# Rows and weights of a feed-forward stage brought in by the stage ahead of it, and its first layer put ahead of its global net

## What is computed

```python
x = x + attn_a(layernorm(x))     # phase A: holographic memory, prefix sums
x = x + ffn(layernorm(x))        # phase F, first time  ("f1")
x = x + attn_b(layernorm(x))     # phase B: hyperbolic Q and K, softmax attention
x = x + ffn(layernorm(x))        # phase F, second time ("f2"), same weights

def ffn(x):
    gf = global_net(x.mean(over rows))        # three small layers, per image
    out = x
    for _ in range(3):
        tf = coupling_net(out)                # 256 -> 256 -> 128 -> 64 -> 1, gelu between
        coupling = 0.1 + adaptive_range * (0.7 * gf + 0.3 * tf - 0.5) * 2
        out = out + coupling * twist(out)
    return out
```

## Time and profile before

| | us |
|---|---|
| three runs | 3031.08, 3026.36, 3031.05 (median 3031.05) |
| the profiled execution | 3026.34 |
| its span in the trace | 3024.6 |
| phase A | 0 to 934.8 |
| phase F, f1 | 934.8 to 1320.9 |
| phase B | 1320.9 to 2636.5 |
| phase F, f2 | 2636.5 to 3024.6 |
| busy: PE / ACT / DVE / POOL | 2724.5 / 2051.4 / 1865.1 / 1231.5 |

### The profile page before, as it was taken

How to read it: one execution, slowest core, us unless ns; L and a number is a source line. 1 busy time by engine, 2 the same in 40 slices (tenths; PEclk the granted TensorE clock), 3 DMA queues, 4 the chain that set the end, 5 groups by cost and what they waited for, 6 DMA issues and landing times. The chain is left out here.

```text
span 3024.6 us, 53754 instructions
## 1 busy us (share of the span) xinstructions
PE 2724.5 (90%) x20801; PEld 1241.0 (41%) x20801; DVE 1865.1 (62%) x2418; ACT 2051.4 (68%) x2696; POOL 1231.5 (41%) x755
## 2 busy tenths in 40 slices
PE   2799999999997999965999999999999999789997
PEld 1455555555554444322333333333333333244443
DVE  8899999999994445456455555555555441144444
ACT  6454454555433555546989898989999999755554
POOL 3788998888893122011414232323232220022100
PEclk7899999999998999977999999999999999999999
DMA  2000010101003021125445455455554546222112
GB/s 84 0 32 25 28 42 24 31 28 32 9 28 106 28 84 55 56 82 112 53 97 90 101 93 105 85 101 97 91 107 78 106 78 123 61 84 70 45 39 70
DMA packets 164051, 201.19 MB, mean 67 GB/s; under 512 B 16505, under 2 KB 118273, under 8 KB 163841
## 3 DMA queue, kind: packets, MB, share of 16 engines
q1 hardware_dynamic: 163840, 198.25, 29.3%
HBM read 139.49 MB, written 58.72 MB: 66 GB/s over the span
## 5 line engine op out<-in xcount | busy, mean ns | idle before, releaser
L1944 ACT ACTIVATE b_pr<-b_ps 128x1024 f32<-128x1024 f32 x1024 | 1000.2, 1035 | 99.2 <-PE b_ps L2012 93.3
L2012 PE MATMUL b_ps<-b_st 128*32 128x512 bf16 x8192 | 627.6, 381 | 43.3 <-ACT b_pr L1944 26.4
L2078 PE MATMUL b_acc<-b_pr,b_vaug 128*32 128x512 f32 x4096 | 542.0, 592 | 3.5 <-DVE b_osb L1773 3.2
L2012 PEld LDWEIGHTS b_ps<-b_st 128*32 128x32 bf16 x8192 | 186.9, 95 | 589.2 <-ACT b_pr L1944 355.0
L1257 PE MATMUL f_po<-f_s,f_w 128*128 128x512 f32 x768 | 353.5, 603 | 9.8 <-DVE f_xr L1042 6.0
L1030 DVE TENSOR_TENSOR f_turned<-f_cs,f_s 128x1024 f32<-128x1024 f32 x96 | 119.1, 1241 | 364.8 <-ACT f_cs L1159 359.3
L635 PE MATMUL a_pv<-a_xnT,a_wv 128*128 128x512 f32 x512 | 251.2, 614 | 52.9 <-DVE a_mem L403 38.7
L1123 ACT ACTIVATE f_h<-f_po,f_b 128x512 f32<-128x512 f32 x192 | 131.9, 687 | 217.0 <-PE f_po L1257 217.0
L627 PE MATMUL a_pu<-a_xnT,a_wk 128*128 128x512 f32 x512 | 238.5, 610 | 29.1 <-DVE a_frac L355 23.2
L1587 POOL TENSOR_TENSOR b_SQ<-b_A 128x1024 f32<-128x1024 f32 x28 | 58.3, 2082 | 438.3 <-DVE b_A L1698 438.3
L674 PE MATMUL a_py<-a_wo,a_out 128*128 128x256 f32 x960 | 229.1, 382 | 0.0
(11 more groups left out here) (283 smaller groups left out, 4545.1 us busy)
## 6 DMA issues: line engine op xcount, KB each, us to landing
b_st<-b_scratch SPq DMA_DIRECT2D x512, 128.0 KB, 7.2
b_scratch<-b_parts SPq DMA_DIRECT2D x32, 768.0 KB, 5.4
f_xl<-x SPq DMA_DIRECT2D x16, 1024.0 KB, 5.5
f_xr<-x SPq DMA_DIRECT2D x16, 1024.0 KB, 6.9
a_xl<-in_L_attn_a_x_dram SPq DMA_DIRECT2D x16, 512.0 KB, 4.3
x<-a_xr SPq DMA_DIRECT2D x32, 256.0 KB, 2.2
x<-f_xr SPq DMA_DIRECT2D x8, 1024.0 KB, 4.5
b_xl<-x SPq DMA_DIRECT2D x8, 1024.0 KB, 8.8
```

The source lines that it names most:

```text
L1944: nc.scalar.activation(pr[:, 4 * (blk % 2) + j, :], ps[:, j % 2, :], ACT.Exp, scale=SC).then_inc(S["probs_done"], 1)
L2012: x = nc.tensor.matmul(o[r:r + 32], w[:, r:r + 32], v, start=start, stop=stop, skip_group_check=True)
L2078: x = nc.tensor.matmul(acc[32 * j:32 * j + 32, h * 512:(h + 1) * 512], vaug[:, kt, c:c + 32], pr[:, 4 * (kt % 2) + j, h * 512:(h + 1) * 51 ...
```

## The change

One class (Front) with shared tiles stands for what a feed-forward stage needs at its start. Seven tiles are allocated once and used by all four phases: big (128 x 4 x 1024; wk_sb and wv_sb in phase A, A in phase B, xl in phase F), weights (128 x 2048; rnd and frac in phase A, EP in phase B, all the weights of phase F), ident, and stats, mv, sm and mhalf.

- **Phase A.** SP, once the last sine is done, issues the 18 loads of weights; once the last products of wk_sb and wv_sb are done, the two loads of rows (images 0 and 1 of x1, stored long before), and then waits for its last stores. DVE, behind L470, takes the statistics of both images and normalises them; POOL, behind its last sum, computes the scales.
- **Phase B.** In the program of the last image SP issues the two loads of rows and the 18 of weights, between the load of xr and the gather for g = 2. DVE takes the statistics in blocks 15 and 16, where the second lies between the two copies of take_acc, and normalises in blocks 21 and 22. POOL computes the scales.
- **Phase F.** Its loads, statistics, scales, normalisation and identity are gone. PE transposes, then does the first layer of image 0 (each tile waits only for the features that it reads and the bank that it writes), and then steps 0, 1 and 2 of the global net, ahead of the second layer. The barrier between the phases stays.
- ident is made once, in phase A; counts on setup_p are lowered for that.

```diff
@@ -51,6 +51,93 @@
...
+class Front:
...
+    def x(self, i):
+        v = self.big[:, 2 * i:2 * i + 2, :].rearrange("p a n -> p (a n)")
+        return v.rearrange("p (t d) -> p t d", t=8)
+
+    def load_rows(self, sp, rows):
+        for x in range(2):
+            sp.dma_start(self.x(x), rows[x]).then_inc(self.x_loaded[x], 16)
+
+    def load_weights(self, sp, loads):
+        for dst, src in loads:
+            sp.dma_start(dst, src).then_inc(self.w_loaded, 16)
+
+    def row_stats(self, nc, dve, x):
+        dve.wait_ge(self.x_loaded[x], 16)
+        for t in range(8):
+            nc.vector.bn_stats(self.stats[:, x, t, :], self.x(x)[:, t, :]).then_inc(self.stats_done, 1)
+        dve.wait_ge(self.stats_done, 8 * (x + 1))
+        for t in range(8):
+            nc.vector.bn_aggr(self.mv[:, x, t, :], self.stats[:, x, t, :]).then_inc(self.mv_done, 1)
+
+    def row_scales(self, nc, pool, x):
+        ve, rstd, nmean = (self.sm[:, i, x] for i in range(3))
+        pool.wait_ge(self.mv_done, 8 * (x + 1))
+        nc.gpsimd.tensor_scalar(ve, self.mv[:, x, :, 1], EPS, None, ALU.add).then_inc(self.rstd_done, 1)
+        nc.gpsimd.tensor_scalar(nmean, self.mv[:, x, :, 0], -1.0, None, ALU.mult).then_inc(self.rstd_done, 1)
+        pool.wait_ge(self.rstd_done, 3 * x + 1)
+        nc.gpsimd.tensor_tensor(rstd, ve, self.mhalf[:, 0:1].broadcast_to([P, 8]), ALU.pow).then_inc(self.rstd_done, 1)
+
+    def row_normalise(self, nc, dve, x):
+        dve.wait_ge(self.rstd_done, 3 * x + 3)
+        for t in range(8):
+            nc.vector.tensor_scalar(self.x(x)[:, t, :], self.x(x)[:, t, :], self.sm[:, 2, x, t:t + 1],
+                                    self.sm[:, 1, x, t:t + 1], ALU.add, ALU.mult).then_inc(self.xn_done, 1)
...
+def ffn_loads(w, cn, gc, arange):
...
+    return [(w["w1"], w1.rearrange("(k p) n -> p k n", p=P)), (w["b1"][:, 0:1], col(b1[0:P])), (w["b1"][:, 1:2], col(b1[P:2 * P])),
+            (w["w2"], w2.rearrange("(k p) n -> p k n", p=P)), (w["w3"], w3),
+            (w["gw1"], gw1.rearrange("(k p) n -> p k n", p=P)), (w["gw2"], gw2),
+            (w["w4c"][0:M3, :], w4), (w["w4c"][M3:P, :], w4), (w["gw3c"][0:M3, :], gw3), (w["b2"], col(b2)),
+            (w["b3"][0:M3, :], col(b3)), (w["b3"][M3:P, :], col(b3)), (w["gb1"], col(gb1)), (w["gb2"][0:M3, :], col(gb2)),
+            (w["sc"][:, 0:1], one(arange)), (w["sc"][:, 5:6], one(b4)), (w["sc"][:, 6:7], one(gb3))]
...
-def phase_a(nc, x_in, wk, wv, wo, gate, freqs, x_out):
+def phase_a(nc, x_in, wk, wv, wo, gate, freqs, x_out, nxt, nxt_loads):
...
-        wk_sb = s.sb("wk", [P, KD, HD])
-        wv_sb = s.sb("wv", [P, KD, HD])
+        wk_sb, wv_sb = nxt.big[:, 0:KD, :], nxt.big[:, KD:2 * KD, :]
...
-        ident = s.sb("ident", [P, P])
+        ident = nxt.ident
...
-        rnd = s.sb("rnd", [P, T])
-        frac = s.sb("frac", [P, T])
+        rnd, frac = nxt.weights[:, 0:T], nxt.weights[:, T:2 * T]
...
                 batch(B - 2)
+                sp.wait_ge(trig_done, NC * B)
+                nxt.load_weights(sp, nxt_loads)
+                sp.wait_ge(u_psum, NC * B)
+                sp.wait_ge(v_psum, 2 * NC * B)
+                nxt.load_rows(sp, [x_out[x].rearrange("(t p) d -> p t d", p=P) for x in range(2)])
...
                 batch(B - 1, last=True)
+                pool.wait_ge(half_done, 1)
+                for x in range(2):
+                    nxt.row_scales(nc, pool, x)
...
                 nc.vector.tensor_tensor(o, o, turn_v[:], ALU.add).then_inc(unit_done, 1)
+                for x in range(2):
+                    nxt.row_stats(nc, dve, x)
+                for x in range(2):
+                    nxt.row_normalise(nc, dve, x)
...
-def phase_f(nc, tag, x_in, x_out, cn, gc, arange):
-    w1, b1, w2, b2, w3, b3, w4, b4 = cn
-    gw1, gb1, gw2, gb2, gw3, gb3 = gc
+def phase_f(nc, tag, x_in, x_out, fr, w):
...
-        xl = s.sb("xl", [P, 2, NT, D])
+        ident, stats, mv, sm, mhalf = fr.ident, fr.stats, fr.mv, fr.sm, fr.mhalf
+        xl = fr.big[:].rearrange("p a n -> p (a n)").rearrange("p (x t d) -> p x t d", x=2, t=NT)
...
-                sp.dma_start(xl[:, 0], xi[0]).then_inc(xl_loaded[0], 16)
-                sp.dma_start(xl[:, 1], xi[1]).then_inc(xl_loaded[1], 16)
-                loads = [
...
-                assert len(loads) * 16 == N_W
-                for dst, src in loads:
-                    sp.dma_start(dst, src).then_inc(w_loaded, 16)
                 sp.dma_start(xr[:, 0], xi[0]).then_inc(xr_loaded, 16)
                 sp.dma_start(xr[:, 1], xi[1]).then_inc(xr_loaded, 16)
...
-                make_identity(nc, pool, ident, setup_p)
                 nc.gpsimd.memset(ones[:], 1.0).then_inc(setup_p, 1)
-                nc.gpsimd.memset(mhalf[:], -0.5).then_inc(setup_p, 1)
...
-                scales(0, 0)
-                scales(1, 0)
                 pair(0, first=True)
...
-                layernorm_stats(0, 0)
-                layernorm_stats(1, 0)
-
-                for x in range(2):
-                    dve.wait_ge(rstd_done, 3 * x + 3)
-                    for t in range(NT):
-                        nc.vector.tensor_scalar(xl[:, x, t, :], xl[:, x, t, :], nmean[:, x, t:t + 1],
-                                                rstd[:, x, t:t + 1], ALU.add, ALU.mult).then_inc(xn_done, 1)
                 nc.vector.memset(sign[0:M3, :], 1.0).then_inc(setup_v, 1)
                 nc.vector.memset(sign[M3:P, :], -1.0).then_inc(setup_v, 1)
                 dve.wait_ge(w_loaded, N_W)
-                dve.wait_ge(setup_p, 4)
+                dve.wait_ge(setup_p, 1)
...
+                        if first and (step, x, k) == ("L1", 0, 0):
+                            act.wait_ge(setup_v, 9)
+                            g_step(0, 0)
+                            g_step(0, 1)
...
-                act.wait_ge(setup_v, 9)
-                g_step(0, 0)
-                g_step(0, 1)
...
                             free(j, at + t, first)
+                            if first and (step, x, k) == ("L1", 0, 0):
+                                pe.wait_ge(act_done, max(3, t + 2))
...
+                        if first and (step, x, k) == ("L1", 0, 0):
+                            pe.wait_ge(act_done, PRO)
+                            pe.wait_ge(setup_v, 9)
+                            g_step(0, 0)
+                            g_step(0, 1)
...
-                pe.wait_ge(setup_p, 2)
...
-                pe.wait_ge(act_done, PRO)
                 pe.wait_ge(w_loaded, N_W)
-                pe.wait_ge(setup_v, 9)
-                g_step(0, 0)
-                g_step(0, 1)
...
+STATS_AT, NORM_AT = (15, 16), (21, 22)
...
-def phase_b(nc, x_in, x_out, zq, bq, zk, bk, wvT, bv):
+def phase_b(nc, x_in, x_out, zq, bq, zk, bk, wvT, bv, nxt, nxt_loads):
...
-        A = s.sb("A", [P, 4, T])
+        A = nxt.big
         SQ = s.sb("SQ", [P, 4, T])
-        EP = s.sb("EP", [P, 2, T])
+        EP = nxt.weights[:].rearrange("p (a n) -> p a n", a=2)
...
+                    if left == 0:
+                        sp.wait_ge(S["fsum_done"], 2 * B)
+                        sp.wait_ge(S["d_done"], 4 * B)
+                        nxt.load_rows(sp, [xo[x] for x in range(2)])
+                        nxt.load_weights(sp, nxt_loads)
                     sp.wait_ge(parts_stored[1], 32 * (b + 1))
...
-                make_identity(nc, pool, ident, S["setup_p"])
...
+                for x in range(2):
+                    nxt.row_scales(nc, pool, x)
...
                         if blk % NT <= 1 and not (first and blk <= 1):
                             take_acc(G * b + blk // NT - 1, blk % NT)
+                        if left == 0 and blk in STATS_AT:
+                            nxt.row_stats(nc, dve, STATS_AT.index(blk))
+                        if left == 0 and blk in NORM_AT:
+                            nxt.row_normalise(nc, dve, NORM_AT.index(blk))
...
-    phase_a(nc, x, *(a["L0_attn_a_" + n] for n in ("Wk", "Wv", "Wo", "gate", "freqs")), x1)
-    phase_f(nc, "f1", x1, x2, cn, gc, a["L0_ffn_adaptive_range"])
-    phase_b(nc, x2, x3, *(a["L0_attn_b_" + n] for n in ("z_q", "b_q", "z_k", "b_k", "w_v", "b_v")))
-    phase_f(nc, "f2", x3, out, cn, gc, a["L0_ffn_adaptive_range"])
+    with Scope(nc, "o") as s:
+        tiles = [s.sb("big", [P, 4, 1024]), s.sb("weights", [P, 2048]), s.sb("ident", [P, P]), s.sb("stats", [P, 2, 8, 6]),
+                 s.sb("mv", [P, 2, 8, 2]), s.sb("sm", [P, 3, 2, 8]), s.sb("mhalf", [P, 1])]
+        f1, f2 = (Front(s, tag, tiles) for tag in ("f1", "f2"))
+        w = ffn_weights(f1.weights)
+        loads = ffn_loads(w, cn, gc, a["L0_ffn_adaptive_range"])
+        phase_a(nc, x, *(a["L0_attn_a_" + n] for n in ("Wk", "Wv", "Wo", "gate", "freqs")), x1, f1, loads)
+        phase_f(nc, "f1", x1, x2, f1, w)
+        phase_b(nc, x2, x3, *(a["L0_attn_b_" + n] for n in ("z_q", "b_q", "z_k", "b_k", "w_v", "b_v")), f2, loads)
+        phase_f(nc, "f2", x3, out, f2, w)
```

85 lines of the change are left out of this document (43 added, 42 removed).

## The result

Four runs of the changed kernel took 2999.87 to 3004.46 us, median 3000.59; the kernel before, with one more run beside them, has a median of 3028.7. The ratio is 0.9915, with a 95% interval from 0.9903 to 0.9927: 25.7 us less of those 3028.7 (the two medians lie 28.1 us apart). The forecast was 3004 with 26.7 us less. The size came out right, and one of its terms did not: what the moved loads cost in phase B was almost four times what the sum had for it.

A forecast was written before the change was run, and what follows sets the result against it. The prediction looked only at the seams between phases, where engines stand in a chain before the second layer. 12.9 (f1) + 16.3 (f2) - 2.3 (gather) - 0.2 (statistics) = 26.7 us, from 3031.05 to 3004.3; range 2993 to 3013.

The forecast's parts named there:

- The chain at the start of a stage: Start of f1 and f2: transposes 5.8, first layer 7.1, global net's steps 2.9; second layer 15.8 us after the phase's start.
- The delay at the end of phase A: Phase A's end: f1's statistics and normalisation now stand there, so f1 starts 3.0 us later, bounds 2.6 to 5.0.
- The clock: After the first layer in f1 and f2: one clock fall in the two stages together, 1.5 us, bounds 0 to 3.
- the 16.3 forecast: Start of f2: 33.61 - 15.8 = 17.8 us won, less 1.5 for the clock, gives 16.3 us.
- The gather behind twenty DMAs: Phase B's last image: 13.1 us of issues delay the gather for g = 2; PE waits 2.3 us, bounds 0 and 5.
- rival 1: Block 16, phase B: the stall takes PE's clock down, costing 3.3 to 4.3 us; time 3008.5, chance 0.14.
- The forecast's own signs of being wrong: Weight issues far from 12 us, low clock in phase B's last image, or a wait for rows after the second layer.
- DVE's statistics between the copies: Phase B's last image: second statistics, 3.8 us, delay the second copy of acc, costing 0.2 us or none.
- Rival 2: No stall at the gather and light stretches at 2.4 GHz: 30.5 us gained, time 3000.5, chance 0.10.
- Rivals 3 and 5: 3: rows late at phase A's end, 3008.3, chance 0.08. 5: stages start no earlier, 3031 to 3036, chance 0.04.
- Rival 4: Phase B from block 16: PE stays at 1.2 GHz after the stall, net loss 25 us, time 3056, chance 0.02.

## Why the forecast was right, and where it was not

**The chain at the start of a stage: right in kind, 1.4 us too long.** 15.8 us were said, 14.36 and 14.45 came. Some of that is luck: both starts of the profiled execution had the early return of the clock, and four of the kernels with the same order had 15.46 to 15.67 us at a start with early loads. The transposes and the first layer are 5.14 and 6.87 us (5.8 and 7.1 said); the global net's row took 951.54 - 949.25 = 2.3 us and not 2.9, with 0.41 and 0.35 us of it waits for ACT's two answers (950.61 and 951.23).

**The delay at the end of phase A: right in kind, a little long.** 3.0 us were said with a lower bound of 2.6; the phase ends 2.34 later, of which 1.7 are the change's. The 18 weights took 9.7 us to issue and not 12.0 (908.04 to 917.7), so DVE, not the rows, set the end, which is the case of the lower bound. Below it the end lies since statistics and normalisation took 936.90 - 924.95 = 11.95 us, and not the 12.73 of the start of f1 before. There DVE stood still four times between its groups, for 0.15, 0.22, 0.15 and 0.26 us, the last time for POOL's scales, and here it did not.

**The clock: right in the mean, and not here.** One fall of 1.5 us in two stages was charged. One of 1.7 us per kernel is what seven kernels show, and none is what the profiled execution of the changed kernel has. Of the 2.9 us by which f2's start beat the 16.3 forecast, 1.5 are that. The reason given, that the row is light work, is incomplete: in seven starts the same row passed without a fall.

**The gather behind twenty DMAs: the step that failed.** 2.3 us were said, with bounds of 0 and 5, and 9.32 came. Two things were wrong. The first is the issue time, which I took from a place where 2 MB stood ahead (13.1 us); with 3 MB it was 18.1, and most of the difference lies in the first three of the 18 loads (6.23 us here, 2.99 at the start of f1 before, 1.69 in the kernel with the weights first). I had named "if the issues take longer with 3 MB in front" as the upper bound and priced it too low. The gather's own time, 16.1 us, was nearly right (2536.97 to about 2552.5, 15.5). The second is the clock: the mechanism of rival 1 came true, after 2.4 us of standing still (from 2552.63 - 6.74 = 2545.89 to 2548.3), and cost 2.6 us, the rest of the 9.32. In the six kernels with a stall and a fall there, the clock fell 2.1 to 4.7 us after PE had stopped. So a wait of 2.3 us, as forecast, might have passed without a fall or not; no run has one between 1.66 us, without a fall, and 4.27, with one. The forecast's own signs of being wrong, issues of the weights that take much more or less than 12 us and a low clock in the last image of phase B, have both come true.

The rule that the time to initiate a DMA is usually small relative to the DMA itself (Trainium skill, DMA: Bandwidth & Descriptors, section Issuing engines are not separate DMA queues) does not hold for these 18 transfers: 10.7 us of issues with 1 MB ahead of them and 16.0 with 3 MB, for 0.6 MB (the five large ones are 576 KB; the 0.7 MB said of them at the start is too much) that would take some 2 us at the rows' 350 GB/s, and at the end of the issues the DMA engines stand at a share of 0.07 (2533 to 2534). The kernel with only the rows ahead is the one where it holds: 2.0 us of issues, and the data decide.

**DVE's statistics between the copies: 0.2 said, nothing seen**, as long as the rows are in. The danger at that place was not the 3.8 us but the wait for the rows in them, which the kernel with the weights ahead turned into 6 us of waiting on PE. The prediction had not named it.

**Rivals.** Rival 1 held in its mechanism, within the forecast's sum only because other terms erred the other way. Rival 2 held for the light rows and failed for the stall. Rivals 3 and 5 are out: DVE has no idle time ahead of its first statistics, and PE starts 0.06 us behind the barrier. Rival 4 is out: the clock was back 6 us after PE had work.

So the sum of 26.7 against 25.8 measured in the traces is a cancellation: -6.8 us in phase B's last image against +1.4 (f1's start), +0.7 (phase A's end), +2.9 (f2's start), -0.8 and +1.6 in the two long stretches between, and +0.2. The 1.6 in phase B ahead of the last image I can't give to the change: the same stretch took 1206.76 to 1212.18 us in the nine other kernels, whatever their edit.

## What to carry to other kernels

A queue that issues DMAs in order has two times that add up: how long the issuing engine is busy, which for these many small transfers was far more than their data and grew with 3 MB ahead of them, and how long the data ahead keep the DMA engines. Put early loads where the issuing engine waits anyway, behind the next transfer that somebody needs, and keep waits for them out of the program of an engine on which a buffer release is queued. A stall forecast at 2 us and more should be priced with the clock's fall as a case of its own (here it came 2.1 to 4.7 us into the stall), and a sum that comes out right should still be checked stretch by stretch. And before an edit gets the credit for a clock that does not fall, compare the clock ahead of the place of the edit: here it told the starts apart.

## What the runs showed of the hardware

- The issue of a 256 KB load took SP 0.53 us with 1 MB under way, 3.57 us with 3 MB, and 8.39 us right behind a gather of 2 MB and 2 MB of rows (the row below). It took 0.43 us in the kernel with only the rows ahead, behind a gather of 2 MB that had itself taken 11.65 us to issue, and not 8.8 as with nothing but xr ahead of it.

```profile
2534.86 8.39 SPq L76 DMA_DIRECT2D o_weights<-in_L_ffn_cn_w_dram  x1
```

- Two executions of nearly the same work differ by some 5 us in stretches that the edits don't touch: phase B ahead of its last image took 1206.76 to 1212.18 us, f1 behind its start took 354.9 to 355.2 us, or 356.8 with the fall of the clock, and phase A's last stores were issued at 929.7 to 930.4 or at 932.0 to 932.6.
